# Reordering the first rounds of a fused three-layer kernel: keys before queries, repeated products of a constant tile between TensorE's steps, copies and a row of scales moved

## What is computed

```
C_q = Q @ Wq_d;  C_kv = K @ Wkv_d                       # Q = layernorm(x), K = context
scores = einsum((C_q @ W_qk) per head, C_kv) / sqrt(32)  # 16 heads of 32
x = x + softmax(scores) @ (C_kv @ Wv_u)

q, k, v = layernorm(x) @ Wqkv + bqkv                     # one head of 128
x = x + softmax(q k / sqrt(128)) @ v @ Wo + bo

xq = 4-bit quantised (layernorm(x) @ hadamard)
wq = ternary_quantize(weight)                            # sign(w) beyond half of the row's mean |w|, times that mean
x = x + xq @ wq.T
```

## Time and profile before

| | before |
|---|---|
| median of three runs | 321.96 us |
| the profiled execution's device time | 320.07 us |
| its span, first to last instruction | 318.1 us |
| TensorE busy | 290.8 us, 91% of the span |
| VectorE busy | 245.5 us, 77% |
| ScalarE busy | 197.0 us, 62% |
| GpSimd busy | 91.2 us, 29% |

### The profile page before, as it was taken

The page is one execution under the profiler, slowest core; times in us unless marked ns, Lnnn a source line. Parts: engine busy times, 40 slices in busy tenths (PEclk is TensorE's granted clock), DMA queues, the critical chain, the costliest instruction groups (busy, mean ns, idle before and its releaser), DMA issues.

```text
span 318.1 us, 11532 instructions
## 1 busy us (share of the span) xinstructions
PE 290.8 (91%) x4602; PEld 204.5 (64%) x4616; DVE 245.5 (77%) x537; ACT 197.0 (62%) x622; POOL 91.2 (29%) x131
## 2 busy tenths in 40 slices
PE   5847989999999999999999999999999989889993
PEld 3535658685858586777768585858586755664641
DVE  1399955879798888889787979787888897884456
ACT  1291926877585949485767677585949485742411
POOL 2103280314233231506060513233241514042410
PEclk9995679999999999999999999999999999999997
DMA  7997230501441322305060506041111101010001
GB/s 226 306 366 293 52 120 2 167 2 40 163 133 71 102 102 73 131 22 180 2 201 3 200 2 197 7 156 47 68 37 34 39 9 59 2 36 2 32 2 66
DMA packets 15813, 29.83 MB, mean 94 GB/s; under 512 B 3472, under 2 KB 4240, under 8 KB 15760
## 3 DMA queue, kind: packets, MB, share of 16 engines
q1 hardware_dynamic: 15760, 29.11, 27.7%
HBM read 24.91 MB, written 4.19 MB: 91 GB/s over the span
## 4 chain that ended last, share of the span: by engine, by line
PE 83%; DVE 8%; issue 3%; ACT 1%; DMA 1%; POOL 1%; SPq 0%; ACTq 0%; DVEq 0%; POOLq 0%
PE ps L951 16%; PE ps L889 10%; PE ps L856 10%; PE ps L845 6%; PE ps L822 5%; PE ps L870 5%; PE ps L902 5%; PE ps L938 5%; PE ps L987 3%; PE ps L809 3%; PE ps L834 3%; PE ps L801 3%; PE ps L880 2%; PE ps L943 2%; DVE mx L560 2%
## 5 line engine op out<-in xcount | busy, mean ns | idle before, releaser
L951 PE MATMUL ps<-had_s,x3t 128*128 128x512 f32 x128 | 59.0, 595 | 1.5 <-ACT x3t L361 1.5
L393 ACT ACTIVATE prob<-ps,nmx,qk_scale 128x128 f32<-128x128 f32 x120 | 53.8, 479 | 0.0
L396 ACT ACTIVATE prob<-ps,nmx,qk_scale 128x128 f32<-128x128 f32 x136 | 51.1, 468 | 0.9 <-DVE nmx L564 0.6
L311 POOL TENSOR_TENSOR rstd<-aux,power 128x1 f32<-128x1 f32 x16 | 8.9, 554 | 139.8 <-DVE aux L618 139.8
L560 DVE TENSOR_REDUCE mx<-ps 128x8 f32<-128x1024 f32 x32 | 39.0, 1217 | 5.1 <-PE ps L845 5.1
L576 DVE STREAM_TRANSPOSE prob_t<-prob 128x1024 f32<-128x1024 f32 x32 | 39.7, 1242 | 0.8 <-ACT prob L393 0.8
L951 PEld LDWEIGHTS ps<-had_s,x3t 128*128 128x128 f32 x128 | 23.6, 190 | 24.3 <-issue 20.6
L856 PE MATMUL ps<-prob_t,ckv_n 32*32 32x128 f32 x2048 | 32.5, 290 | 3.6 <-issue 2.3
L889 PE MATMUL ps<-x2t,wqkv_s 128*128 128x128 f32 x256 | 34.2, 287 | 0.7 <-issue 0.4
L889 PEld LDWEIGHTS ps<-x2t,wqkv_s 128*128 128x128 f32 x256 | 31.0, 197 | 4.7 <-issue 3.5
L856 PEld LDWEIGHTS ps<-prob_t,ckv_n 32*32 32x32 f32 x2048 | 25.4, 105 | 9.9 <-issue 7.9
(11 more groups left out here) (121 smaller groups left out, 549.6 us busy)
## 6 DMA issues: line engine op xcount, KB each, us to landing
ct<-ctx_cols SPq DMA_DIRECT2D x16, 512.0 KB, 5.4
xt<-x_cols SPq DMA_DIRECT2D x16, 256.0 KB, 3.3
xs<-x_rows SPq DMA_DIRECT2D x16, 256.0 KB, 5.3
xr<-x_rows SPq DMA_DIRECT2D x16, 256.0 KB, 2.7
y<-res SPq DMA_DIRECT2D x15, 256.0 KB, 3.1
w_rows<-weight SPq DMA_DIRECT2D x1, 1024.0 KB, 8.3
had_s<-hadamard SPq DMA_DIRECT2D x1, 1024.0 KB, 8.5
wqkv_s<-wqkv SPq DMA_DIRECT2D x1, 768.0 KB, 10.1
```

The costliest lines, as they stand in the source:

```text
L393: last = nc.scalar.activation(prob[:, h, :], score, ACT.Exp, bias=nmx[:, h:h + 1], scale=scale, accum_out=sum_a[:, h:h + 1])
L396: last = nc.scalar.activation(prob[:, h, :], score, ACT.Exp, bias=nmx[:, h:h + 1], scale=scale)
L951: mm = pe.matmul(ps[:, b2(n), :], x3t[:, c, :], had_s[:, c, :], start=(c == 0), stop=(c == EC - 1))
```

## The change

The list of each engine is written in another order for pairs 0 to 2, and a helper `warm(n)` is added to TensorE: n products of `mean_w` with itself into bank B1. No result of them is read. There are 33 of them, in nine places.

- Loads: the context of pair 0 is issued ahead of x of pair 0. TensorE takes `ckvp(0)` ahead of `cq(0)`, and the semaphore of the pair is then set by `cq(0)`. The product with `wq_raw` goes to bank B2 in place of B4, and TensorE waits for `wq_c` only ahead of `cq(0)`.
- TensorE: `qt(0)` and `scores(0)` come ahead of `cq(1)`; `wide_scale` goes from ahead of `weighted(0)` to behind `cq(3)`.
- ScalarE: `exps(0, 0, 8)` comes ahead of `latc(1)`, and `ckc(1)` goes between two parts of `exps(0, 8, 16)`; `scale_copy` goes behind `exps(1)`.
- VectorE: `turned(0, 0)` comes ahead of `wabs`, `turned(0, 1)` ahead of `wscale` and `ternary(0)`; `ternary(1)` and `ternary(2)` go behind `largest(1, 0)` and `largest(1, 1)`.

```diff
-            load_cols(0)
+            sp.dma_start(ct[:, 0], ctx_cols[0]).then_inc(ld_ct[0], 16)
+            sp.dma_start(xt[:, 0], x_cols[0]).then_inc(ld_xt[0], 16)
...
-            latc(0); ckc(0); qtc(0); latc(1); ckc(1); exps(0, 0, 8); exps(0, 8, 16); qtc(1); latc(2); utc(0); ckc(2)
-            scale_copy(); exps(1, 0, 8); exps(1, 8, 16); qtc(2); latc(3); hadamard_mean(); ternary_copy(0); x2tc(0)
+            latc(0); ckc(0); qtc(0); exps(0, 0, 8); latc(1); exps(0, 8, 12); ckc(1); exps(0, 12, 16); qtc(1); latc(2); utc(0); ckc(2)
+            exps(1, 0, 8); exps(1, 8, 16); scale_copy(); qtc(2); latc(3); hadamard_mean(); ternary_copy(0); x2tc(0)
...
-            st1(0); st1(1); largest(0, 0); largest(0, 1); ckvT(0); wabs(); turned(0, 0); wscale(); ternary(0)
-            turned(0, 1); ternary(1); sums(0); rsums(0); ternary(2); largest(1, 0); largest(1, 1); st1(2)
+            st1(0); st1(1); largest(0, 0); largest(0, 1); ckvT(0); turned(0, 0); wabs(); turned(0, 1);
+            wscale(); ternary(0); sums(0); rsums(0)
+            largest(1, 0); largest(1, 1); ternary(1); ternary(2); st1(2)
...
+            def warm(n):
+
+                for _ in range(n):
+                    pe.matmul(ps[:, B1, 0:P], mean_w[:], mean_w[:], start=True, stop=True)
+
+            warm(4)
             pe.wait_ge(ld_w["wq"], 16)
...
-            pe.wait_ge(wq_ready, 1)
...
             def cq(n):
+                if n == 0:
+                    pe.wait_ge(wq_ready, 1)
...
+                if n == 0:
+                    mm.then_inc(made["lat"], 1)
...
-            cq(0); ckvp(0); foldkv(0); cq(1); qt(0); ckvp(1); scores(0); foldkv(1); cq(2); qt(1); ckvp(2)
-            wide_scale(); weighted(0); scores(1); foldkv(2); xo(0); cq(3); qt(2); ckvp(3); hadamard_mean()
+            warm(3); ckvp(0); cq(0); warm(2); foldkv(0); warm(1); qt(0); warm(2); scores(0); cq(1); ckvp(1);
+            warm(12); foldkv(1); cq(2); qt(1); ckvp(2); warm(2); weighted(0); warm(2); scores(1);
+            foldkv(2); xo(0); cq(3); wide_scale(); warm(5); qt(2); ckvp(3); hadamard_mean()
```

More of the change, by code:

```diff
@@ L509, in _ @@
             dve.wait_ge(ld_w["wq"], 16)
-            V.tensor_tensor(wq_c[:], wq_raw[:], ps[:, B4, 0:LQ].unsqueeze(1).to_broadcast([P, EC, LQ]),
+            V.tensor_tensor(wq_c[:], wq_raw[:], ps[:, B2, 0:LQ].unsqueeze(1).to_broadcast([P, EC, LQ]),
                             ALU.subtract).then_inc(wq_ready, 1)
@@ L750, in _ @@
             pe.wait_ge(consts_set, 4)
+            def warm(n):
+                for _ in range(n):
+                    pe.matmul(ps[:, B1, 0:P], mean_w[:], mean_w[:], start=True, stop=True)
+            warm(4)
             pe.wait_ge(ld_w["wq"], 16)
             for c in range(EC):
-                mm = pe.matmul(ps[:, B4, 0:LQ], mean_w[:], wq_raw[:, c, :], start=(c == 0), stop=(c == EC - 1))
+                mm = pe.matmul(ps[:, B2, 0:LQ], mean_w[:], wq_raw[:, c, :], start=(c == 0), stop=(c == EC - 1))
             mm.then_inc(mean_made, 1)
             pe.wait_ge(ident_set, 4)
-            pe.wait_ge(wq_ready, 1)
             def wide_bias():
@@ L800, in cq @@
                         c = 2 * t + h
-                        pe.matmul(ps[64 * t:64 * t + 64, B4, 0:P], wq_c[:, c, :], xt[:, n % 2, c, :],
-                                  start=(h == 0), stop=(h == 1))
+                        mm = pe.matmul(ps[64 * t:64 * t + 64, B4, 0:P], wq_c[:, c, :], xt[:, n % 2, c, :],
+                                       start=(h == 0), stop=(h == 1))
+                if n == 0:
+                    mm.then_inc(made["lat"], 1)
             def ckvp(n):
@@ L810, in ckvp @@
                                    start=True, stop=True)
-                mm.then_inc(made["lat"], 1)
+                if n:
+                    mm.then_inc(made["lat"], 1)
             def qt(n):
```

## The result

The changed kernel takes 325.64 us in the median of four runs (323.06 to 326.38). The kernel before now has a fourth run beside them and takes 321.27 us in the median of the four. The ratio of the runs is 1.0104, with a 95% interval of 1.0061 to 1.0148; the two medians alone give 1.014. The forecast was 320.2 us, at most 323.0. The profiled execution took 326.38 us, 6.3 us more than that of before.

A forecast was written before the change was run, and what follows sets the result against it. TensorE was taken to bound the kernel. +1.05 us for VectorE, -3.2 for `weighted(1)` to `scores(2)` and +0.3 for the next block gave -1.8, so 321.96 becomes 320.2 us; range 318.0 to 323.0.

The forecast's parts named there:

- What bounds the kernel, and that the first rounds' date passes on whole: TensorE, 91% busy, 83% of the chain; time saved or lost before `scores(2)` starts reaches the end nearly whole.
- Pair 0 up to its scores: First TensorE chain up to `scores(0)`: ends at 13.1 us with the clock risen, against 14.87 before.
- VectorE takes most of this back: VectorE up to `xmul(0)`: GpSimd's sum holds `ternary(0)` and one more ternary part is added, so 1.05 us later.
- `weighted(1)` to `scores(2)`: TensorE stretch: 3.9 instead of 7.07 us, saving 3.2 us from a 1.44 us gap and the lower clock behind it.
- The small gap foreseen in `qk(0)`: The next instruction block's boundary falls late in `qk(0)`; 0.3 us allowed.
- Rival 2: Late instruction block 42 records into `scores(1)`: 321.5 us if mild, 323.8 if full; chance 0.23 (0.15 and 0.08).
- From there all as before: All rounds after `scores(2)`, expected near 46.6 us, run as in the kernel before, 1.8 us earlier.
- gaps that before's do not have: Sign that the forecast is wrong: the later rounds get gaps absent in the kernel before.
- Rival 1: TensorE's clock falls in the wait for `xmul(0)`, making `weighted(1)` late by 0.9 us: 321.1 us; chance 0.17.
- Rivals 3 and 4: 3: the 1.44 us gap in `weighted(1)` stays, 323.0 us, chance 0.07. 4: more is gained, 318.0 us, chance 0.15.

The follow-up runs named there:

- few_then_116: Changed order, but only 6 products (24 records, four products wide) ahead of `scores(1)` and 116 additional records in all; 0.9952 of the kernel before.
- after_again: The changed kernel itself, profiled and timed once more; 1.0102 of the kernel before.
- many_then_116: Changed kernel without 4 of the 5 products ahead of `qt(2)`, 116 additional records, 112 of them ahead of `scores(1)`; 0.9997 of the kernel before.
- total_148: Changed kernel with four products more behind `wide_scale`, 148 additional records; 1.0065 of the kernel before.
- few_then_132: As `few_then_116`, with 4 small products more, so 132 additional records as in the changed kernel; 1.0000 of the kernel before.
- products_only: Order of the kernel before, with the 33 products put in comparable places in TensorE's waits; 1.0017 of the kernel before.

## Why the prediction was wrong, step by step

- **What bounds the kernel, and that the first rounds' date passes on whole:** the bound was right: TensorE is in 81% of the chain after, too. That the later rounds stay as they were was not.
- **Pair 0 up to its scores, 13.1 us:** 13.40. The exponentials end at 22.1 (22.2), `weighted(0)` starts at 23.54 and takes 1.90 us (23.5, 1.90). Right.
- **VectorE takes most of this back, +1.05 us, because GpSimd holds `ternary(0)`:** wrong in this execution. The matrix landed at 24.75 instead of 23.13, `ternary(0)` had started 0.27 us ahead of GpSimd's sum and took its 0.75 us, and `sums(0)` started at 25.15 instead of 27.5. In `few_then_116` the ternary part started 0.20 us behind the sum (24.61 against 24.41) and took 2.72 us, `sums(0)` starts at 27.26, and the rest of the step comes out within 0.2 us. The term depends on when a DMA lands, by some tenths of a us, and can fall away; here that gained nothing, because VectorE then waited for `scores(1)`.
- **`weighted(1)` to `scores(2)`, 3.9 instead of 7.07 us:** 4.22 (45.12 to 49.34). The gap was the end of a block, as argued, and the products moved it away. The small gap foreseen in `qk(0)` is there, 0.26 us for an allowed 0.3.
- **Rival 2, the late block in `scores(1)`, 42 records in:** this is what happened, 44 records in, at 26.88 us for an estimated 26.4. The packet ran at 27.4, where the text gave 1.3 us as the price for 27.3. The chance, 0.23, looks too low, since the gap came again in every kernel with this front (3.08 us in `after_again` and `many_then_116`), and the price was too low by half: `scores(2)` came 2.7 us after the forecast's 46.6. The text let `scores(1)` have slack up to 29.1 us and go on 2.3 us after the packet at full speed. It went on after 2.6 us, and its last 42 matmuls took 1.56 us at the lower clock.
- **"From there all as before":** the step that failed most, 5.6 of the 8.3 us between the forecast's span (316.3) and the measured one. The forecast took the shift by 132 records to the next end of a block and stopped there. The grid runs through all 16 rounds, and each of its 36 ends moves. The trace of before held what was needed to find the places: the step of 250 from 939 to 2192 (the 256 that the prediction got from 9,218 over 36 is near it by chance, for the steps measure 250.7), the number of records in a round, `weighted` with its 256 records in 1.9 us, and packet to work in 2.3 us, which is longer. Counting on would have found records 3450 and 7462 as the ones at risk. It would have given gaps of about 1.9 and 1.5 us, not the clock's share. The prediction did name "gaps that before's do not have" as a sign of being wrong, at no price.
- **Rival 1, the clock:** it was 0.50 in 32 to 36 us, but as a follower of the gap, not of the wait for `xmul(0)`. What wasn't considered at all is that a gap in the steady rounds can bring the clock down too; in this kernel it did both times, and doubled their cost.
- **Rivals 3 and 4** did not occur.

## What to carry to other kernels

Adding or removing instructions on a long straight program moves every later instruction against the blocks in which they are fetched. Dummy work that fills a pause is not free even if its time is: count the records up to the ends of the blocks, in all rounds, and look which block is used up fastest, above all where bulk transfers run. Try two or three neighbouring counts before judging such an edit: with otherwise the same order 100, 116, 132 and 148 additional records gave 1.011, 1.000, 1.010 and 1.007. And read the clock behind each gap, for the count alone doesn't set the price: 132 records in another order gave 1.000 and 1.002.

## What was not expected of the hardware

- TensorE's 250 records of `weighted` are used up in 1.9 us, faster than the next block arrives (2.4 to 3.3 us after its packet), although its packet runs one block ahead.
- Beside bulk loads the gap behind record 692 took 3.08 us, without them 0.61.
- Gaps of about the same length in a dense stretch brought the granted clock down in some kernels and not in others: it fell behind 1.19 us (`total_148`), 1.52 and 1.88 us (after), and stayed at 1.00 behind 1.33 (`many_then_116`), 1.50 and 1.81 (`few_then_132`) and 1.82 us (`products_only`). A fall cost the round about 1.5 us more.
- VectorE's ternary part took 0.75 us when it started 0.27 us ahead of GpSimd's sum and 2.72 us when it started 0.20 us behind; it then ended at 27.33, 0.5 us after the sum (24.41 and 2.38 us). So it was held until the sum was done rather than slowed by a share: in `few_then_132` a scaling of 128x4, 0.13 us in after, took 2.30 us and ended with the sum.

**Open.** Why some packets come later than the rule without traffic isn't settled: in before one ran 9.3 us after the block was entered, with a DMA share of 0.02 from 30 to 37 us, and in after, pairing packets with ends in order, some seven of 35 ran 2 to 6 us after beside a share under 0.1. What decides whether the clock falls behind a gap is open too, and with it a good part of the 1%. Nor is it shown whether any of these kernels beats before: `few_then_116` gave 0.9952 once and 1.0002 the second time.
